# Cross attention in a fused decoder layer: values of two units at once over four column groups, and a new order of values, maxima and context keys

## What is computed

```python
def _L0_xattn_ref(x, context, w_qkv, w_proj, b_proj):
    H = 16; D = C // H                       # 16 heads of 8
    q, k, v = ...                            # from x @ w_qkv.T
    extra_k, extra_v = ...                   # from context
    k = jnp.concatenate([extra_k, k], axis=2)
    v = jnp.concatenate([extra_v, v], axis=2)
    attn = jax.nn.softmax(jnp.einsum('bhnd,bhmd->bhnm', q * scale, k), axis=-1)
    out = jnp.einsum('bhnm,bhmd->bhnd', attn, v)
    return out.transpose(0, 2, 1, 3).reshape(B, N, C) @ w_proj.T + b_proj

x = x + _L0_attn_ref(_layernorm(x), ...)
x = x + _L0_xattn_ref(_layernorm(x), ctx_2048, ...)
x = x + _L0_ffn_ref(_layernorm(x), ...)
```

## Time and profile before

| | us |
|---|---|
| median of 3 runs | 1043.14 |
| lowest, highest | 1042.57, 1044.83 |
| the profiled execution | 1034.5 |
| its span | 1032.8 |

### The profile page before, as it was taken

The page is one execution under the profiler, slowest core; times in us unless marked ns, Lnnn a source line. Parts: engine busy times, 40 slices in busy tenths (PEclk is TensorE's granted clock), DMA queues, the critical chain, the costliest instruction groups (busy, mean ns, idle before and its releaser), DMA issues.

```text
span 1032.8 us, 29894 instructions
## 1 busy us (share of the span) xinstructions
PE 872.2 (84%) x11671; PEld 693.9 (67%) x11671; DVE 760.5 (74%) x1899; ACT 604.3 (59%) x1391; POOL 525.4 (51%) x909
## 2 busy tenths in 40 slices
PE   4899999999999999698888888888888855777760
PEld 3688888888888888566666666666666634665640
DVE  4888888888888888577778778778778746655552
ACT  2567767777777667466666566666666523544430
POOL 4444444444444445334444754754754654566661
PEclk9999999999999999989999999999999985998985
DMA  8980000000000000000000100100104002223316
GB/s 202 162 199 2 2 2 2 3 1 2 2 2 3 1 3 2 11 12 12 12 17 13 33 23 15 33 20 15 33 19 132 28 16 79 71 75 103 104 36 175
DMA packets 54655, 43.33 MB, mean 42 GB/s; under 512 B 10163, under 2 KB 48362, under 8 KB 54516
## 3 DMA queue, kind: packets, MB, share of 16 engines
q1 hardware_dynamic: 49568, 32.97, 13.5%
q0 software_dynamic: 4608, 8.30, 2.6%
q10 hardware_dynamic: 340, 0.14, 0.1%
HBM read 21.46 MB, written 21.12 MB: 41 GB/s over the span
## 4 chain that ended last, share of the span: by engine, by line
PE 57%; DVE 25%; issue 9%; ACT 3%; DMA 2%; another core or an unknown queue 2%; POOL 1%; DVEq 0%; SPq 0%; POOLq 0%; ACTq 0%
PE ps L1174 48%; DVE nmax L1037 10%; PE ps L1225 7%; DVE kT L937 2%; DVE q_part L937 2%; DMA w_qkv<-in_L_attn_W_v 1%; DMA raw_gu<-y_part 1%; DVE bst L1063 1%; DVE padded L1081 1%; DVE bst L1056 1%; DVE zT L1029 1%; ACT xT_hi L727 1%; DVE padded L1078 1%; DVE w_qkv L1149 1%
## 5 line engine op out<-in xcount | busy, mean ns | idle before, releaser
L1037 DVE TENSOR_REDUCE nmax<-ps 128x2 f32<-128x512 f32 x256 | 163.9, 683 | 36.6 <-PE ps L1174 35.7
L734 ACT ACTIVATE probsT<-ps 128x512 f32<-128x512 f32 x256 | 139.5, 601 | 58.7 <-PE ps L1174 56.6
L661 ACT ACTIVATE probs<-ps,nmax 128x128 f32<-128x128 f32 x512 | 142.9, 383 | 10.4 <-DVE nmax L801 10.1
L1174 PE MATMUL ps<-probsT,va 128*32 128x128 f32 x2048 | 138.4, 277 | 5.3 <-ACT zT L739 4.8
L495 POOL TENSOR_TENSOR probs<-probs,rinv 128x512 f32<-128x512 f32 x128 | 133.0, 1039 | 18.8 <-DVE rinv L811 18.8
L655 ACT COPY probsT<-ps 128x512 f32<-128x512 f32 x128 | 75.1, 587 | 84.9 <-PE ps L1225 84.8
L1174 PEld LDWEIGHTS ps<-probsT,va 128*32 128x32 f32 x2048 | 104.2, 110 | 23.7 <-issue 16.6
L626 POOL DMA_INDIRECT y_part<-wo_all,slot_ids x80 | 81.1, 1014 | 57.4 <-DVE wo_all L1128 32.2
L801 DVE TENSOR_REDUCE nmax<-ps 128x4 f32<-128x512 f32 x128 | 83.5, 673 | 35.5 <-PE ps L1174 35.4
L1174 PE MATMUL ps<-xT_hi,w 128*128 128x128 f16 x1024 | 98.7, 222 | 6.4 <-DVE raw_gu L845 4.4
L1174 PE MATMUL ps<-xT_lo,w 128*128 128x128 f16 x512 | 91.3, 222 | 0.0
(11 more groups left out here) (224 smaller groups left out, 2235.3 us busy)
## 6 DMA issues: line engine op xcount, KB each, us to landing
slots<-blank SPq DMA_DIRECT2D x1, 5200.0 KB, 43.7
w<-slots SPq DMA_DIRECT2D x16, 325.0 KB
y_part<-blank SPq DMA_DIRECT2D x2, 2048.0 KB, 31.9
ctx_row<-in_ctx SPq DMA_DIRECT2D x32, 128.0 KB
raw_gu<-y_part SPq DMA_DIRECT2D x16, 256.0 KB
out_x<-x_all SPq DMA_DIRECT2D x8, 256.0 KB, 3.9
y_part<-wo_all,slot_ids POOLq DMA_INDIRECT x80
slots<-rows,slot POOLq DMA_INDIRECT x64
```

Source lines behind the costliest of these rows:

```text
L661: last = nc.scalar.activation(probs[:, u, i * P:(i + 1) * P], ps[u][:, i * P:(i + 1) * P], ACT.Exp, bias=nmax[:, u, i:i + 1])
L734: last = nc.scalar.activation(probsT[:, 2 * (t % 2) + a, :], ps[2 + a][:, :], ACT.Exp)
L1037: last = nc.vector.reduce_max(nmax2[:, b % 2, t:t + 2, l + a], ps[a][:, :].rearrange("p (t k) -> p t k", t=2), AX_X, negate=True)
L1174: return nc.tensor.matmul(o, l, r, start=start, stop=stop, **kw)
```

## The change

The exponentials of a sequence's four units now have a place each (exp_cells: units 0 and 1 in probsT, units 2 and 3 in probs, which self attention no longer needs). apply_values works on a pair of units: for each t and k it issues four matmuls, one for each of the four column groups, and is called twice a sequence. It stands at g = 2 for the first pair, behind the transposed scores, and at g = 0 of the following step for the second pair, between the query projection and the shift. The context keys' matmuls move on PE from g = 2, ahead of the transpose of xn3, to g = 3, ahead of the value projection; ScalarE's copy of them moves with them. The waits that count ca_values_applied are changed to two a sequence. In self attention VectorE's xn moves ahead of the two evictions of keys. The number of matmuls and of all other work stays the same.

```diff
+        exp_cells = [[(probsT, probs)[u // 2][:, 2 * (u % 2) + a, :] for a in range(2)] for u in range(UNITS)]
...
@@ gpsimd
                         if valid(-2):
-                            pool.wait_ge(ca_values_applied, UNITS * (b - 2) + UNITS)
+                            pool.wait_ge(ca_values_applied, 2 * (b - 2) + 2)
...
@@ scalar
-                    if g == 2 and valid(1):
+                    if g == 3 and valid(1):
                         n = b + 1
                         act.wait_ge(ca_keys_in_bank, n + 1)
...
                     if valid(-1):
-                        t = UNITS * (b - 1) + g
-                        act.wait_ge(ca_scores_T, t + 1)
-                        if t >= 2:
-                            act.wait_ge(ca_values_applied, t - 1)
+                        act.wait_ge(ca_scores_T, UNITS * (b - 1) + g + 1)
+                        if valid(-2):
+                            act.wait_ge(ca_values_applied, 2 * (b - 2) + g // 2 + 1)
                         for a in range(2):
-                            last = nc.scalar.activation(probsT[:, 2 * (t % 2) + a, :], ps[2 + a][:, :], ACT.Exp)
+                            last = nc.scalar.activation(exp_cells[g][a], ps[2 + a][:, :], ACT.Exp)
                         last.then_inc(ca_exp, 1)
                     if g == 0 and valid(-2):
                         n = b - 2
-                        act.wait_ge(ca_values_applied, UNITS * n + UNITS)
+                        act.wait_ge(ca_values_applied, 2 * n + 2)
                         nc.scalar.copy(z_aug, ps[4][:, :]).then_inc(ca_z_taken, 1)
...
@@ vector, self_attention
+                    if g == 1 and valid(2):
+                        n = b + 2
+                        dve.wait_ge(sa_rstd, n + 1)
+                        nc.vector.tensor_scalar(xn[:, :], x_all[:, n, :], mv[:, 0, 0:1], rstd[:, 0:1],
+                                                ALU.subtract, ALU.mult).then_inc(sa_norm, 1)
+
                     if valid(1) and g < 2:
...
-                        if g == 1:
-                            dve.wait_ge(sa_rstd, n + 1)
-                            nc.vector.tensor_scalar(xn[:, :], x_all[:, n, :], mv[:, 0, 0:1], rstd[:, 0:1],
-                                                    ALU.subtract, ALU.mult).then_inc(sa_norm, 1)
...
@@ tensor
-            def apply_values(n, u):
-                pe.wait_ge(ca_exp, UNITS * n + u + 1)
-                if u == 0:
+            def apply_values(n, pair):
+                pe.wait_ge(ca_exp, UNITS * n + 2 * pair + 2)
+                if pair == 0:
...
-                buf = 2 * ((UNITS * n + u) % 2)
-                for t in (2 * (u // 2), 2 * (u // 2) + 1):
+                for t in (2 * pair, 2 * pair + 1):
                     for k in range(2):
-                        for a in range(2):
-                            l = 2 * (u % 2) + a
+                        for l in range(4):
                             last = mm(ps[4][ROWS * l:ROWS * l + ROWS, t * P:(t + 1) * P], va[:, n % 3, k, 4 * t + l, :],
-                                      probsT[:, buf + a, (2 * (t % 2) + k) * P:(2 * (t % 2) + k + 1) * P],
+                                      exp_cells[2 * pair + l // 2][l % 2][:, (2 * (t % 2) + k) * P:(2 * (t % 2) + k + 1) * P],
                                       k == 0, k == 1)
...
                         last.then_inc(ca_q_in_bank, 1)
+                    if g == 0 and valid(-2):
+                        apply_values(b - 2, 1)
                     if g == 0 and valid(-1):
                         pe.wait_ge(ca_max_padded, b)
...
                         last.then_inc(ca_zq_in_bank, 1)
-                    if g == 2 and valid(1):
+                    if g == 2 and valid(-3):
+                        pe.wait_ge(ff_norm, b - 2)
+                        pe.wait_ge(ca_residual, b - 2)
+                        nc.tensor.transpose(ps[7][:, 2 * P:3 * P], xn3[:, :], ident[:, :]).then_inc(ff_xT_in_bank, 1)
+                    if g == 3 and valid(1):
                         pe.wait_ge(ca_context_keys, n + 1)
                         pe.wait_ge(ca_k_packed, n + 1)
...
-                    if g == 2 and valid(-3):
-                        pe.wait_ge(ff_norm, b - 2)
-                        pe.wait_ge(ca_residual, b - 2)
-                        nc.tensor.transpose(ps[7][:, 2 * P:3 * P], xn3[:, :], ident[:, :]).then_inc(ff_xT_in_bank, 1)
...
                     if valid(0):
                         scores(b, g)
-                    if g == 0 and valid(-2):
-                        apply_values(b - 2, UNITS - 1)
                     if valid(-1):
                         transposed_scores(b - 1, g)
-                        if g > 0:
-                            apply_values(b - 1, g - 1)
+                        if g == 2:
+                            apply_values(b - 1, 0)
```

## The result

The median lies 2 us above my range: 1076.9 us (1073.0 to 1078.9, 4 runs) against 1042.9 for the kernel before (1040.4 to 1044.8, 4 runs beside them). The ratio is 1.034 (95% interval 1.031 to 1.037), slower, where I had forecast 1056 and a range of 1031 to 1075. So the two traces differ by 41.5 us, the medians by 34.

The account below looks back on a forecast made before the run. Cross attention was taken as a chain of waits, with PE on it between keys and zn. 11 us gained by the new order and 24 lost to clock falls gave +13 on 1043.1: 1056 us, range 1031 to 1075.

Parts of the forecast that it names:

- the end steps: Cross attention steps 1, 2, 30, 31 and the two behind: 0.7 us gained each, 4.2 in all (bounds 1 and 8).
- the start: Start of self attention: PE gets xn 1.2 us earlier, 1.2 us gained (bounds 0 and 2).
- Walk of a plain step: Cross attention steps without scatters or routing: zn earlier, xT2_lo at +8.11 not +8.48; 0.37 us gained each, 3.3 over nine.
- rival 2: Value bursts: four column groups run no faster than two, 1.9 us a burst, 1074 us in all; chance 0.07.
- the estimate of 0.2 more: Value bursts: by the Trainium skill's measured speedup, a burst of four column groups would be about 0.2 us longer.
- The routing steps: Eight cross attention steps in which routing work adds to VectorE: 0.3 us gained each, 2.4 in all.
- The moved keys: Context keys one unit later: PE's 0.65 us wait for packed keys goes; the later start costs nothing.
- Scatter steps: Ten cross attention steps with scatter DMAs: xn2 transposed at +8.09 as before, gain 0, cover for the values used up.
- if a burst holds the shift: Sign of being wrong, ahead of the shift: VectorE's 1.32 us wait before its first maxima would grow.
- The clock's price: Cross attention: PE's hole before xn3 lowers the clock in three steps of four; 21 us plus 3 for longer falls, 24.
- Rival 1: Cross attention: the clock holds at its full level, everything else as forecast; 1032 us (1028 to 1040), chance 0.31.
- rival 3: Cross attention: the clock falls in only one step in three, -11 + 10, about 1042 us, no change; chance 0.09.

Follow-up runs that it names:

- e1: The changed kernel with 24 idle identity matmuls a step on PE behind the transposes of z, ahead of the wait for xn3; 0.998 of the kernel before.
- e9: e1 with each value burst doing the 16 records of column groups 0 and 1 for both tiles before those of groups 2 and 3; 1.015 of the kernel before.
- e3: The kernel before with only self attention's xn moved ahead of the two key evictions on VectorE; 0.999 of the kernel before.
- e5: The kernel before with the context half of unit 0's values left out (4 matmuls, 0.44 us a step); 1.021 of the kernel before.
- e6: e1 with the value bursts changing between pairs of column groups after every fourth matmul; 0.998 of the kernel before.
- e11: The changed kernel with the values of units 2 and 3 behind the shift, output projection and first scores, no work added; 1.012 of the kernel before.

## Why the prediction was right or wrong

The forecast was slower, by the clock, and that is what happened; it was 21 us short, between medians. The steps that failed are two: the price of a fall, which I put at 24 us in all where the stage shows 35.5, and the end steps, to which I gave a gain and which lost. Term by term, with the two profiled runs (41.5 us apart, forecast 13): in the stage I had -8.5 for the order and +24 for the clock, and the traces show -1.3 (e1 against before) and +35.5 (after against e1), together +34.2. For the start I had -1.2 and it was +0.9; for the two steps behind the stage I had -1.4, and all that follows the stage is 6.4 longer.

**Walk of a plain step: right.** Behind the transposes of z PE stands 2.1 us for xn3 (forecast +2.85 to +4.86, 2.0 us), the 0.65 us ahead of the keys is gone, a burst has 1.08 us (forecast 1.1; neither rival 2's 1.9 nor the estimate of 0.2 more came). With the clock held the plain steps take 11.65 (forecast 11.7). All nine save 1.9 us in e1, where 3.3 was forecast; the missing 1.4 is one fall, in step 26 (13.43 us, 12.06 in its like). The routing steps save 3.3 us in all (forecast 2.4). The moved keys: 0.3 a step, as walked.

**Scatter steps: nearly.** Forecast 0 gained; with the clock held each of ten costs 0.1 more on the mean, in some 0.25. How that comes is below.

**End steps: wrong.** Of the 4.2 us of my sum 2.8 fall to the four steps in the stage, 0.7 gained in each. In e1 they lose 2.9 us together. In steps 2 and 31 (a step is named by the padded column that it starts with) the values hold the shift, by 0.6 and 0.5 us, which the busier VectorE of the other steps covers. e1's step 31, VectorE and PE, at the full clock:
```profile
815.68 0.20 DVE L1081 TENSOR_SCALAR padded<-nmax 128x16 f16<-128x16 f32 x1
```
```profile
815.68 1.08 PE L1177 MATMUL ps<-probs,va 128*32 128x128 f32 x32 [1.25 <-ACT probs L735]
816.70 0.23 PE L1177 MATMUL ps<-ident_h,padded 128*128 128x128 f16 x1
```
The shift starts 1.02 us behind the first padded column, where in before it starts 0.52 behind (816.24 and 816.76). Behind the stage the same wait is 1.3 us in e1 (828.18 to 829.47, part of it at the lower clock) and 0.5 in before. The other 1.8 us of the loss are not taken apart by any run: in step 1 the clock of e1 comes back at 455.9, that of before at 449.6, and in step 31 e1 has a fall (12.50 us; e9, which has none, takes 12.01). I had named a held shift ("if a burst holds the shift") as a thing that would make me wrong and then given the end steps the gain of a step in which it is covered. The term is off by 5.7 us. All in all the order was worth 1.3 us in the stage of e1, not 8.5.

**The clock's price: mechanism right, size wrong.** I had falls in three steps of four, 1.5 us in a plain step, 0.8, 0.45 and 1.0 in the others, and 3 us for long ones: 24. Against e1 the stage of after is 35.5 us longer: 13.7 in the plain steps, 13.2 in the routing, 6.4 in the scatter and 2.2 in the end steps. Four things were mis-sized. There were 28 falls in 31 steps, not 23. I let the low stretch end with zn; 11 times it ran on over the second burst and the shift, for which VectorE stood 3.13 us in the step shown, not 1.66, and which made a plain step 3.0 us longer than 11.7, not 1.5. A plain step with a short fall alone lost 1.0 us, and the nine together 1.7 on the mean (against their like without a fall), not 0.75 x 1.5 = 1.1. The routing steps were furthest off: 1.7 us on the mean, not 0.75 x 0.8 = 0.6, and 3.0 in the four that a long fall reaches, so that VectorE's routing work doesn't cover it. The scatter steps, to which I had given their slack ahead of xn2 as cover, pay 0.6 on the mean (6.4 over ten), not 0.34; that this slack covers the chain and not the shift is my reading.

**The tail: not in the sum.** Behind the last padded column after takes 6.4 us longer. Its clock is low without a break from 843.6 to 905, through the last burst, the weights' transposes and the first experts; before had its full clock back at 866, but for 7 us from 869.5. That the cause is the fall at the end of the stage fits the other kernels only loosely (tails of 204 to 212 us; e1, with its clock held in the stage, has 209.4 where before has 205.1), and no run took it apart.

**The start: 1.2 us of gain forecast, none seen**, and none could be read (e3).

**Rivals.** Rival 1 (the clock holds) was refuted for this kernel, but e1 shows that I would have been wrong there too: 1041, not 1032. Rival 2's condition, a burst of more than 1.1 us, didn't come true, nor did rival 3's few falls. The chances: I gave 0.34 to faster on the strength of a clock that had been at its full level all through the stage; the row that weighed more was 1.81 us of standing at 828.21 with 0.51 behind it, the same size as the hole that I had forecast.

The Trainium skill (TensorE: Matmul & The Clock Gate, A second HAM failure mode: psum-queue depth-cycling) describes a kernel in which PE idles briefly between groups of matmuls, so that the clock goes down and up again and the change is paid between bursts. The trace agrees, with 28 falls in 31 steps; here the idle stretches are 2.0 us, and idle matmuls put into them undid nearly all falls (e1, 3 left).

## What to carry to other kernels

Before taking work off an engine whose clock follows its load, walk the step and ask where it will stand instead: if nothing on the other engines gets shorter, the saved time becomes a hole, and a hole can cost more than the work did. Less work made this kernel 2% slower (e5), and idle matmuls gave the changed kernel back all that it had lost (e1), so idle matmuls in the hole are the cheapest test of such a theory. Price a low clock to the end of what is still running at it, the next burst and the next shift included, and walk the first and last steps on their own: in two of four the cover of the steady steps was missing here.

## What the runs showed that I had not expected

Column groups needn't be issued four at a time to overlap. With groups 0 and 1 alternating for four matmuls and then 2 and 3 (e6), 32 records took 1.10 us, as with four at once (1.08); only both tiles of a pair in a row (e9) made it 1.54.

In scatter steps of the new order ScalarE starts q_shifted late: 0.75 us behind the shift's last matmul in e1, 0.5 in after, against 0.04 in all of before and in the other steps (0.21 in e1's step 31). ScalarE, GpSimd and PE of one such step of e1:
```profile
805.79 0.59 ACT L707 CAST q_shifted<-ps 128x512 f16<-128x512 f32 x1 [1.89 <-PE ps L1177]
```
```profile
804.40 1.02 POOL L588 DMA_INDIRECT slots<-rows,slot  x1 [0.15 <-issue]
805.42 0.31 POOL L525 COPY va<-ctx_row 128x128 f32<-128x128 f32 x1
```
```profile
804.79 0.22 PE L1177 MATMUL ps<-q_part,ident_h 128*128 128x128 f16 x1
```
The shift is done at 805.01. VectorE pays for it too: in these steps of e1 it stands 1.53 to 1.56 us ahead of its first maxima, not 1.32, and that is nearly the 0.25 us of the scatter steps above. As far as the traces show, it happens where GpSimd, which waits for the values' signal to copy the next context values (L525), is sent that signal while it is generating a scatter, though not each time. In e1's eight late steps ScalarE starts 0.34 to 0.38 us behind the end of the scatter, in after's seven 0.42 to 0.50. Before has a scatter in the same place (from 0.6 us ahead of the shift's end), but its values end later, and none of its ten is late; nor is one in e11, where the values come behind the shift. So it takes both, the scatter and the signal. Why PE's next signal to another engine should be held up by that is open; no run separates it further.
